# Summing the three component products of a message on TensorE instead of VectorE, in the second layer of a graph network

## The reference

```
R   = relu(abs_distances[:, None] @ w1 + b1) @ w2 + b2         # 384 radial weights of an edge
Y   = spherical_harmonics(rel_vec)                             # of l = 0, 1, 2
Fj  = features[src]                                            # 8 scalars and 8 vectors of 3
for i, (mo, lo) in enumerate(RS):                              # RS = [(8, 0), (8, 1)]
    acc = zeros(E, mo, 2 * lo + 1)
    for j, (mi, li) in enumerate(RS):
        for k, lf in enumerate(range(abs(lo - li), lo + li + 1)):
            acc += _NORM[i] * einsum('euv,ef,evi,ofi->euo', Rb[..., k], Yf, Fb, C)
    msg_blocks.append(acc.reshape(E, -1))
msg = concatenate(msg_blocks)                                  # 8 + 24 = 32 columns
out = zeros.at[dst].add(msg)
```

## Time and profile before

| | us |
|---|---|
| median of 3 runs | 20244.84 |
| lowest and highest run | 20231.5, 20246.46 |
| profiled execution | 20216.02 |
| its span, first to last instruction | 20214.2 |
| second layer in it, first gather to last transpose of messages | 7041.2 to 11417.0 |

### The profile page before, as it was taken

One profiled execution on the slowest core, in us unless ns is written; L12 is line 12 of the kernel. 1 busy time (PEld: TensorE's weight loads), 2 busy tenths in 40 slices (PEclk: granted clock), 3 DMA queues, 4 the chain that ended last, 5 costly groups with the idle time before them and its releaser, 6 DMA issues. The chain is left out here.

```text
span 20214.2 us, 339137 instructions
## 1 busy us (share of the span) xinstructions
PE 13896.3 (69%) x116979; PEld 7785.7 (39%) x116979; DVE 11289.5 (56%) x19866; ACT 3016.9 (15%) x4900; POOL 11914.2 (59%) x10098
## 2 busy tenths in 40 slices
PE   0466555555555388888888446666666499999999
PEld 0244343333333255555555212222222255455554
DVE  2675544444444399999999623333333345555554
ACT  0022222222222111111111111111111000000000
POOL 4488888888888577777777577777777200000000
PEclk6665555555555599999999767777777799999999
DMA  5444444444444322222222145555555245555555
GB/s 178 147 40 37 38 38 38 37 37 37 37 38 37 40 61 62 63 63 63 63 63 62 40 70 89 89 88 89 89 88 89 75 155 198 198 194 200 196 201 175
DMA packets 3692951, 1821.96 MB, mean 90 GB/s; under 512 B 2869044, under 2 KB 3476094, under 8 KB 3676958
## 3 DMA queue, kind: packets, MB, share of 16 engines
q1 hardware_dynamic: 1754910, 1394.80, 24.9%
q0 software_dynamic: 670464, 169.16, 10.3%
q10 hardware_dynamic: 1266578, 244.09, 7.6%
HBM read 1476.78 MB, written 394.51 MB: 93 GB/s over the span
## 5 line engine op out<-in xcount | busy, mean ns | idle before, releaser
L2816 PE MATMUL pacc<-nodes,HB 128*32 128x512 fp8e4 x70560 | 3933.9, 380 | 282.6 <-PEq L2860 281.4
L1961 POOL DMA_INDIRECT xg<-d_tab,s_i x3136 | 3345.4, 1067 | 1172.3 <-issue 864.5
L2450 POOL DMA_INDIRECT xg<-d_tab,s_i x3136 | 3008.1, 959 | 969.9 <-issue 903.7
L2207 PE MATMUL pR<-w,H 128*128 128x384 f32 x6272 | 2369.5, 500 | 770.6 <-PEq L2201 770.5
L1413 POOL DMA_INDIRECT d_acc<-T,ix x1568 | 2471.2, 1576 | 520.5 <-issue 451.0
L1413 POOL DMA_INDIRECT d_acc<-AG,ix x1568 | 2469.6, 1575 | 518.8 <-issue 423.5
L2816 PEld LDWEIGHTS pacc<-nodes,HB 128*32 128x32 bf16 x70560 | 1904.9, 97 | 2184.4 <-issue 300.6
L1768 PE MATMUL pm<-ms,eq 128*128 128x32 f32 x6272 | 1365.4, 399 | 926.8 <-PEq L1766 926.8
L2785 DVE TENSOR_SCALAR nodes<-packed 128x1792 int32<-128x1792 int32 x900 | 944.3, 1049 | 1818.5 <-DVEq L2783 1818.5
L2478 DVE TENSOR_TENSOR_SCAN U<-mU,U,up 128x512 f32<-128x512 f32 x392 | 501.7, 1280 | 2434.7 <-DVEq L2477 2429.9
L2207 PEld LDWEIGHTS pR<-w,H 128*128 128x128 f32 x6272 | 1064.1, 189 | 1746.7 <-issue 1325.8
(11 more groups left out here) (346 smaller groups left out, 18326.1 us busy)
## 6 DMA issues: line engine op xcount, KB each, us to landing
packed<-d_A SPq DMA_DIRECT2D x420, 1792.0 KB, 7.5
row<-d_m SPq DMA_DIRECT2D x1568, 64.0 KB
wrow<-d_w SPq DMA_DIRECT2D x196, 512.0 KB, 5.2
xg<-d_tab,s_i POOLq DMA_INDIRECT x6272
d_scan<-so ACTq DMA_DIRECT2D x392, 256.0 KB
d_A<-stage ACTq DMA_DIRECT2D x96, 784.0 KB
d_exp<-zt SPq DMA_DIRECT2D x32, 1568.0 KB, 19.6
xe<-d_exp SPq DMA_DIRECT2D x196, 256.0 KB
```

The costliest lines, as they stand in the source:

```text
L1961: e.indirect_dma_start(out=xg[k][:, t, :], out_offset=None, in_=d_tab, in_offset=bass.IndirectOffsetOnAxis(ap=s_i[n][:, t:t + 1], axis=0)) ...
L2207: last = e.matmul(pR[u % 2][:, j, 0:384], H[k][:, (2 * u + j) * P:(2 * u + j + 1) * P], w2[:, :], start=True, stop=True)
L2450: e.indirect_dma_start(out=xg[n][:, j * ST + c, :], out_offset=None, in_=d_tab, in_offset=bass.IndirectOffsetOnAxis(ap=s_i[d][:, col:col + ...
L2816: end = e.matmul(pacc[k][32 * g:32 * (g + 1), :], HB[i][:, b0 + bb, 32 * h:32 * (h + 1)], of, start=(begins and h == 0), stop=(ends and h ...
```

## The change

VectorE makes no sum over the three components any more. `tail` writes each component's product to its own plane of `tv`, in the order of columns that `mg` had; the 8 scalars go to plane 0, and the same columns of planes 1 and 2 are zeroed once before the loop. `columns` then accumulates, for each of its four blocks, three ordinary products of a plane with the identity in PSUM, where it made one transpose. `mg` and its semaphore `fmg` are gone; `tv` has one buffer.

```diff
-            mg = [sb(st, f"mg{k}", [P, T, F]) for k in range(2)]
-            tv = sb(st, "tv", [P, 3, T, 8, 3])
+            tv = sb(st, "tv", [P, 3, T, F])
 ...
-                    for k in range(2):
-                        e.sem_inc(S(f"fmg{k}"), 1)
+                    e.memset(tv[:, 1:3, :, 0:8], 0.0).then_inc(S("vc"), 1)
+                    e.wait_ge(S("vc"), 1)
+                    e.sem_inc(S("vc"), -1)
 ...
                         if part == 0:
                             e.wait_ge(S("vq"), 3)
                             e.sem_inc(S("vq"), -3)
-                            e.wait_ge(S(f"fmg{k}"), 1)
-                            e.sem_inc(S(f"fmg{k}"), -1)
-                            e.tensor_copy(by_stream(mg[k])[:, :, :, 0:8],
+                            e.tensor_copy(by_stream(tv[:, 0, :, :])[:, :, :, 0:8],
                                           Q[k][:, 0, :, :].rearrange("p (c j) u -> p c j u", c=ST))
-                            e.tensor_tensor(tv[:, :, :, :, :], bc(Q[k][:, 1:4, :, :], 4, 3), bc(e9[n][:, :, :, :], 3, 8),
-                                            ALU.mult).then_inc(S("tz"), 1)
-                        elif part == 1:
-                            e.wait_ge(S("tz"), 1)
-                            e.sem_inc(S("tz"), -1)
-                            e.tensor_tensor(tv[:, 0, :, :, :], tv[:, 0, :, :, :], tv[:, 1, :, :, :], ALU.add
-                                            ).then_inc(S("tz"), 1)
-                        else:
-                            e.wait_ge(S("tz"), 1)
-                            e.sem_inc(S("tz"), -1)
-                            of = tv[:, :, :, :, :].rearrange("p k (c j) u o -> p k c j (u o)", c=ST)
-                            e.tensor_tensor(by_stream(mg[k])[:, :, :, 8:32], of[:, 0, :, :, :], of[:, 2, :, :, :], ALU.add
-                                            ).then_inc(S(f"mg{k}"), 1)
+                        last = e.tensor_tensor(by_stream(tv[:, part, :, :])[:, :, :, 8:32]
+                                               .rearrange("p c j (u o) -> p c j u o", o=3),
+                                               bc(Q[k][:, 1 + part, :, :].rearrange("p (c j) u -> p c j u", c=ST), 4, 3),
+                                               bc(e9[n][:, part, :, :].rearrange("p (c j) o -> p c j o", c=ST), 3, 8), ALU.mult)
+                        if part == 2:
+                            last.then_inc(S(f"mg{k}"), 1)
 ...
                     def scan(n):
                         scan_dve(e, b, n, tp[n % 2][:, :], ALU.mult, ALU.add)
-                        e.sem_inc(S(f"fmg{n % 2}"), 1)
 ...
                         for j in range(CH):
-                            last = e.transpose(tp[k][:, j * P:(j + 1) * P],
-                                               mg[k][:, j * ST:(j + 1) * ST, :].rearrange("p c f -> p (c f)"), ident[:, :])
+                            for i in range(3):
+                                last = e.matmul(tp[k][:, j * P:(j + 1) * P],
+                                                tv[:, i, j * ST:(j + 1) * ST, :].rearrange("p c f -> p (c f)"), ident[:, :],
+                                                start=(i == 0), stop=(i == 2))
                         last.then_inc(S("tp"), 1)
```

More of the change, by code:

```diff
@@ L1894, in by_stream @@
             def by_stream(of):
-                return of[:, :, :].rearrange("p (j c) x -> p c j x", c=ST)
+                return of.rearrange("p (j c) x -> p c j x", c=ST)
             with nc.Block() as block:
```

## The result

| | before | after |
|---|---|---|
| median, us | 20238.17 (4 runs) | 20356.05 (4 runs) |
| lowest and highest run | 20195.06, 20246.46 | 20352.26, 20358.14 |
| ratio to before, 95% interval | | 1.0062, 1.0045 to 1.008 |
| span of the profiled execution | 20214.2 | 20355.6 |

The change makes the kernel slower by 0.6%. The forecast was 20410, 0.8% slower, with a range of 20320 to 20515.

The account below looks back on a forecast made before the run. Before, GpSimd's gathers set the 22.11 us step, VectorE 0.5 us behind; after, a TensorE-VectorE loop: 20.65 - 0.39 + 2.69 = 22.95 us. The extra 0.84 us in 196 steps is 165 us, median 20410, range 20320 to 20515.

Parts of the forecast that it names:

- GpSimd's 22.13 us: Gathers before the change: sixteen at 1.068 us plus 0.315 between them, so GpSimd never rests in the layer.
- The loop: From products of u = 1 through radial 3 to 5 and back on VectorE: 20.65 us before, 22.95 after.
- the eight sums: Each half of `early_sums` on TensorE, between radials 3 and 4 and before `columns`: 2.13 us, counted twice.
- The wait ahead of u = 5: VectorE's wait for radial 5 in front of L2029 after the change: 2.11 us in every step.
- the 8.97: Time in us after u = 1 at which VectorE alone would reach u = 5; radial 5 admits it at 11.08.
- The gain of 0.80: VectorE's saving per step in us, at least 0.44, from three multiplications of 384 elements; said to lie outside the loop.
- 5.61 with 6.68: Times in us after u = 1: last multiplication ends at 5.61, TensorE reaches `columns` at 6.68, so `columns` doesn't wait.
- The worst case of 22.85 us: GpSimd's step after the change: 16 x 1.25 = 20.0 us plus 2.85 of gathers held up by VectorE.
- The rule of the Trainium skill: `tensor_tensor` doesn't hold up descriptor generation, so removing VectorE work would give GpSimd nothing; the prediction cited 3.02 us against it.
- The one that goes by TensorE's idle time: TensorE's added work is hidden in its 18% idle, 20067 us; decides if 24 records take under 1.85 us; chance 0.07.
- That a product costs four transposes: Products in `columns` at 0.39 us each, twelve 4.66 us, loop 24.92 us, time 20796 us; chance 0.03.
- The second stall, at radial 6: Radial 6 or 7 late, or 3.02 us gathers every step: step 23.3 to 24 us, 20480 to 20615; chance 0.09.

Follow-up runs that it names:

- e9: Kernel before the change with fifteen gathers a step instead of sixteen; 20133 us, 0.9945 of before, step 21.63 us.
- e2: Kernel before with TensorE's part alone: twelve identity products in `columns`, VectorE's work kept; 20467 us, 1.0112 of before, step 23.27 us.
- e10: Changed kernel with fifteen gathers a step instead of sixteen; 20338 us, 1.0048 of before, step 22.67 us.
- e5: Changed kernel with two planes in `columns`, eight products instead of twelve; 20154 us, 0.9957 of before, step 21.77 us.
- e8: Kernel before with `head`'s three multiplications spread over u = 2, 3 and 4; 20251 us, 1.001 of before, step 22.26 us.
- e4: Changed kernel with `columns`, all twelve products, moved behind radial 6; 20138 us, 0.9951 of before, step 21.53 us.
- e3: Changed kernel with `columns` transposing plane 0 alone, so VectorE's part without TensorE's; 20099 us, 0.993 of before, step 21.33 us.
- e1: Changed kernel with the `tz` wait on the previous part of `tail` put back; 20346 us in one run, step 22.67 us.

## Why the prediction was right

**What bounds the kernel.** That GpSimd held the layer, 0.46 us above VectorE, is shown by e9, which gained 0.46 a step. One correction: GpSimd's 22.13 us are not a cost of its own, and that it never rests doesn't show that it binds. With fifteen gathers their mean length rose from 1.068 to 1.142 us, and 15 x (1.142 + 0.305) = 21.7, so GpSimd rests nowhere in e9 either, though VectorE waits for nothing there. A gather above 2.5 us stands 82 times in the 196 steps before and 197 times in those of e9, where each step has the same three that are held up:

```profile
9041.53 1.32 POOL L1961 DMA_INDIRECT xg<-d_tab,s_i  x1 [0.30 <-issue]
9043.15 3.03 POOL L1961 DMA_INDIRECT xg<-d_tab,s_i  x1 [0.30 <-issue]
9046.48 1.38 POOL L1961 DMA_INDIRECT xg<-d_tab,s_i  x1 [0.30 <-issue]
```

GpSimd and VectorE hold each other up, and taking 1.38 us from one gave 0.46. What shows the bound is the wait in `head` and its end in e9, not GpSimd's full row.

**The loop.** Right in its course and in all terms but one, which stands in it twice. By the rows above, with the forecast in brackets: from the end of u = 1 at 9030.77 + 0.75 = 9031.52 to radial 3 0.26 (0.26); radial 3 1.07 (1.08); sums 2.00 (2.13); radial 4 1.08 (1.08); sums 2.00 (2.13); `columns` 2.68 (2.69); from radial 5's weight load at 9040.61 to the products of u = 5 at 9042.32 1.71 (1.57 + 0.14). On VectorE, from 9042.32 to the end of u = 1 in the next step at 9053.45 + 0.74, it is 11.87 (11.87). These add up to 22.67, and the step is 22.68.

**The term that was off** is the eight sums, 2.13 for 2.00, twice: 0.26 of 22.95 us a step, 51 us in all. I read it off a step in which radial 4 did not start when TensorE was free, but when VectorE's queue let it, as the 0.41 us above suggest, and then used the same number for the second half, where nothing showed it. The trace of before had the right number, which I didn't set down in the sum: in the last step of the layer, where the message was there in time, the second half of the sums and `columns` begin 2.00 apart.

```profile
11399.03 2.08 PEld L2213 LDWEIGHTS pQ<-PP,ident 128*128 128x128 f32 x16
11401.03 0.47 PEld L2237 LDWEIGHTS tp<-ident,mg 128*128 128x128 f32 x4
```

With 2.00 twice the sum is 22.69, and the step is 22.68. The wait ahead of u = 5 was forecast as 2.11 and measured as 1.71. Of the difference, 0.28 is radial 5, which came earlier (10.80 after u = 1 for 11.08). The other 0.12 is mostly that the 8.97 ran to where the next instruction would start, while idle time counts from the end of the last one, which lies some 0.1 later.

**VectorE's part.** The gain of 0.80 is right (0.47 for a multiplication of 384 elements, the lower of my two values). The sentence that it "lies outside the loop" is only true of the changed kernel. Where the 0.80 are not saved, the second arm over `tail` and `columns` closes later and the step is 0.59 longer (e2). I had compared 5.61 with 6.68 and stopped; the comparison with L2064 at its old place, 5.61 + 0.80 = 6.41 and then the time from its end to `columns`, would have given the second arm. That time stood in the earlier trace rows: 9033.84 to 9034.41, 0.57. Over this arm the loop before was 6.41 + 0.57 + 0.39 + 1.71 + 11.87 = 20.95 and not 20.65, so its room under the step was 1.1 us and not 1.5, and TensorE's 2.29 less 1.1 are the 1.18 that e2 lost.

**GpSimd.** The worst case of 22.85 us did not come into play (e10). Gathers wait for `fxg` now, as forecast: 168.4 us ahead of 168 of them between 7200 and 11200, where 47.6 us ahead of 156 were the usual 0.3 each. The rule of the Trainium skill by which `tensor_tensor` doesn't hold up descriptor generation (page "SBUF — State Buffer", section Who interferes with whom) can't be carried over to a whole gather here. In the step of the changed kernel that is shown above, a gather begins under the second multiplication of `tail` (9033.23), which `head` follows (9033.69 to 9035.49):

```profile
9033.24 3.05 POOL L1960 DMA_INDIRECT xg<-d_tab,s_i  x1 [0.30 <-issue]
```

It ends 0.8 us after `head`. What part of a gather is held up, no run shows, so for descriptor generation by itself the rule stays open.

**The rivals.** The one that goes by TensorE's idle time is what the wrong forecast would have been. Its point of decision, the 24 records in under 1.85 us, was 0.24 too low, for the same reason: without `columns` the loop is 22.68 - 2.68 = 20.00, which leaves 2.09 under the step before. e5, with sixteen records in 16 x 0.112 = 1.79 us, is on the fast side of either. That a product costs four transposes is out (2.68 us for twelve). The second stall, at radial 6, didn't come.

## What to carry to other kernels

Read an engine's room not from its idle share but from the loop it stands in: follow from the work that waits, back through the other engine's program order, to where the loop closes, and compare its length with the step. Work that is moved onto an engine with time to spare belongs behind the instruction that somebody waits for next; here its place behind radial 6 instead of ahead of radial 5 turned 0.6% of loss into 0.5% of gain. An engine that never rests isn't thereby the one that binds: its work can be stretched by the one that does, as in e9. And when a term is read from a row, look at whether that instruction was free to start or was let in by a token; the same term from a step where it was free is the one that survives the change.

## What the runs showed that was not expected

- A gather on GpSimd is held up by VectorE's two-input instructions in SBUF for as long as these follow each other, and cutting them into pieces moves the time without removing it (e8): the longest 3.06 to 1.93 us, the mean 1.068 to 1.080.
- A shorter list of gathers makes each longer, 1.068 to 1.142 us, as the same places of every step hold them up. VectorE's records grow too, by about 0.034 us each in the mean (output AG of L2029 before and L2033 in e9 from 685 to 719 ns, the scan from 1275 to 1309). Why, no run shows; the step is VectorE's 21.63 all the same.
- Stages that a kernel doesn't change start up to 49 us apart between executions (first weight load of `columns` at 7108.5 in e4 and 7157.9 in e3). A difference of 0.2% in the total has to be looked for in the layer, where the changed kernel, e1 and e10, which differ in nothing that binds, have steps of 22.67 to 22.68 us.
